# A transformer block with a state-space mixer and a quantised FFN on one core: another order of the steps on three engines, and the last down product in two halves of columns

## What is computed

```
sa, ca, ga, sb, cb, gb = six sections of (silu(c) @ w_mod)      # ga, gb kept at least 0.25 away from 0
h = layernorm(x) * (1 + ca) + sa
x = x + ga * mixer(h)
h = layernorm(x) * (1 + cb) + sb
return x + gb * ffn(h)

mixer(h):  z, xBC, dt = split(h @ W_in.T)            # 1024, 1280 and 16 columns
           dt = softplus(dt + dt_bias)
           x, B, C = split(silu(causal conv of 4 taps over xBC))      # 16 heads of 64; B, C of 128
           y = scan of the state S <- exp(dt*A)*S + dt*B*x, read out by C, plus D*x
           y = y * silu(z);  y = y * rsqrt(mean(y*y) + 1e-5) * norm_w
           return y @ W_out.T
ffn(h):    return (silu(h @ Wg.T) * (h @ Wu.T)) @ Wd.T     # 1408 hidden columns, integer weights with scales
```

## Time and profile before

| | |
|---|---|
| median of 3 runs | 1406.8 us (1405.69 to 1407.49) |
| profiled execution | 1406.29 us, of which the span of its trace is 1404.4 us |
| granted TensorE clock, mean | 0.994 |
| busy: PE, PEld, DVE, ACT, POOL | 99%, 84%, 76%, 55%, 13% |

### The profile page before, as it was taken

The page is one execution under the profiler, slowest core; times in us unless marked ns, Lnnn a source line. Parts: engine busy times, 40 slices in busy tenths (PEclk is TensorE's granted clock), DMA queues, the critical chain, the costliest instruction groups (busy, mean ns, idle before and its releaser), DMA issues.

```text
span 1404.4 us, 26004 instructions
## 1 busy us (share of the span) xinstructions
PE 1385.7 (99%) x9607; PEld 1173.2 (84%) x9607; DVE 1071.5 (76%) x2095; ACT 777.4 (55%) x1782; POOL 185.1 (13%) x270
## 2 busy tenths in 40 slices
PE   8899999999999999999999999999999999999998
PEld 6788888888888888888888888798888888888887
DVE  4888899999999989989989988766645536464542
ACT  5867777787787787787787787522211112021110
POOL 0011111111111111101111111111020110102101
PEclk8999999999999999999999999999999999999999
DMA  8422123223124223122332234522020201202010
GB/s 289 170 79 98 69 100 106 84 89 116 61 77 140 73 76 126 72 91 85 98 106 83 92 98 140 222 98 75 1 90 15 75 31 61 90 0 91 15 45 31
DMA packets 61066, 125.02 MB, mean 89 GB/s; under 512 B 6998, under 2 KB 10626, under 8 KB 60940
## 3 DMA queue, kind: packets, MB, share of 16 engines
q1 hardware_dynamic: 60112, 122.22, 25.4%
q10 hardware_dynamic: 828, 1.12, 0.2%
HBM read 97.62 MB, written 25.69 MB: 88 GB/s over the span
## 4 chain that ended last, share of the span: by engine, by line
PE 90%; issue 4%; DMA 2%; DVE 2%; POOL 1%; ACT 1%; SPq 0%; POOLq 0%; ACTq 0%; DVEq 0%
PE bank L1563 29%; PE bank L2153 19%; PE bank L2183 9%; PE bank L1714 9%; PE bank L56 5%; PE bank L1718 4%; PE bank L1685 4%; PE bank L1649 4%; PE bank L1693 2%; PE bank L1629 2%; PE bank L1553 1%; PE bank L2134 1%; DMA silu_z<-W_inT 1%; POOL ff_x_resid L1980 1%; DMA ff_x_resid<-x_scratch 0%
## 5 line engine op out<-in xcount | busy, mean ns | idle before, releaser
L1988 ACT ACTIVATE silu_gate<-bank,params 128x512 f32<-128x512 f32 (+1 forms) x99 | 63.5, 642 | 363.3 <-PE bank L2153 343.9
L1074 DVE SCALAR_TENSOR_TENSOR xBC<-conv_in,wconv,xBC 128x256 f32<-128x256 f32 x480 | 223.1, 476 | 10.5 <-ACT xBC L782 8.0
L2060 DVE SCALAR_TENSOR_TENSOR hidden<-bank,params,silu_gate 128x512 f32<-128x512 f32 (+1 forms) x99 | 68.3, 690 | 126.7 <-PE bank L2153 126.7
L857 ACT ACTIVATE decay<-decay,sums 128x128 f32<-128x128 f32 x512 | 156.5, 395 | 0.2 <-DMA decay<-sums_scratch 0.2
L2183 PE MATMUL bank<-W_down,hidden_high 128*128 128x512 f32 x374 | 138.9, 390 | 0.0
L2153 PE MATMUL bank<-ff_h_high,W_gate 128*128 128x512 f32 (+1 forms) x352 | 132.1, 379 | 0.0
L700 POOL TENSOR_TENSOR X_D<-X,Drow 128x1024 f32<-128x1024 f32 x32 | 61.7, 1927 | 532.4 <-ACT X_D L871 290.1
L2153 PE MATMUL bank<-ff_h_high,W_up 128*128 128x512 f32 (+1 forms) x352 | 130.9, 376 | 0.3 <-DVE hidden L2060 0.3
L2153 PE MATMUL bank<-ff_h_low,W_gate 128*128 128x512 f32 (+1 forms) x352 | 130.9, 376 | 0.0
L2153 PE MATMUL bank<-ff_h_low,W_up 128*128 128x512 f32 (+1 forms) x352 | 130.9, 376 | 0.0
L2183 PE MATMUL bank<-W_down,hidden_low 128*128 128x512 f32 x330 | 128.4, 389 | 0.0
(11 more groups left out here) (199 smaller groups left out, 3118.4 us busy)
## 6 DMA issues: line engine op xcount, KB each, us to landing
decay<-sums_scratch SPq DMA_DIRECT2D x62, 512.0 KB, 4.8
wq_rows<-wqT SPq DMA_DIRECT2D x33, 256.0 KB, 2.9
widened_scratch<-wq_rows SPq DMA_DIRECT2D x33, 256.0 KB, 2.0
x_tile<-x SPq DMA_DIRECT2D x32, 256.0 KB, 3.3
x_resid<-x SPq DMA_DIRECT2D x32, 256.0 KB, 2.8
x_scratch<-x_resid SPq DMA_DIRECT2D x32, 256.0 KB, 2.0
ff_x_resid<-x_scratch SPq DMA_DIRECT2D x32, 256.0 KB, 4.4
out<-ff_x_resid SPq DMA_DIRECT2D x32, 256.0 KB, 2.0
```

The costliest lines, as they stand in the source:

```text
L857: last = nc.scalar.activation(x[:, h, :], x[:, h, :], ACT.Relu, bias=A.s3[:, o:o + 1], scale=-1.0)
L1074: nc.vector.scalar_tensor_tensor(A.xc[b][:, m, :], A.raw[:, m, j:j + SC], A.wconv[:, m, j:j + 1], A.xc[b][:, m, :], ALU.mult, ALU.add).the ...
L1988: self.nc.scalar.activation(B.sg[m % 2][:, 0:size], self.gates[m % 2][:, 0:size], ACT.Silu, scale=self.T.sgate[:, m:m + 1]).then_inc(self. ...
L2060: nc.vector.scalar_tensor_tensor(hid, self.ups[m % 2][:, 0:size], self.T.sup[:, m:m + 1], B.sg[m % 2][:, 0:size], ALU.mult, ALU.mult).then ...
```

## The change

The three tables get another order in `first()`, `turn()` and `drain()` of TensorE, VectorE and ScalarE; no step is added or dropped in them. In the FFN the last tile of `down` (turn 8, c = 3) is done in two halves of 256 columns, first into bank 7, then into bank 6, with twice as many matmuls of half the width. For this tile VectorE also adds the residual, in place of GpSimd, and SP makes two stores of 128 KB in place of one of 256 KB.

```diff
@@ tensor, first() @@
             n, b = 0, 0
+            setup.turn_params(pe)
             project_zdt(n, 0)
-            setup.turn_params(pe)
             project_zdt(n, 1)
...
             project_tile(n, 9)
-            cumulate(n)
             pe.wait_ge(setup.win_low, len(setup.stage))
             project_z(n, 0)
             project_z(n, 1)
+            cumulate(n)
@@ tensor, drain() @@
             project(0, 3)
+            states(n, u, 0, 0)
             project(0, 4)
-            states(n, u, 0, 0)
             states(n, u, 0, 1)
@@ vector, drain() @@
+            decay_S(u, b, 0, 1)
+            decay_S(u, b, 1, 1)
+            decay_S(u, b, 1, 0)
+            decay_X(n, u, 0)
             gate(n, u, b, 0)
             ff.hidden(dve, 0, 2)
-            decay_X(n, u, 0)
-            decay_S(u, b, 0, 1)
@@ FFN @@
+    def last(self, t, c):
+        return t == self.N - 1 and c == self.NC[t] - 1
+
+    def pieces(self, t, c):
+        D = self.T.D
+        return (slice(0, D // 2), slice(D // 2, D)) if self.last(t, c) else (slice(0, D),)
@@ sync @@
-                wait(sp, self.summed, self.first[t] + c, 1, 1)
-                sp.dma_start(self.rows_of(T.out, t, c), B.xr[c][:]).then_inc(self.out_sent[c], 16)
+                for h, s in enumerate(self.pieces(t, c)):
+                    if self.last(t, c):
+                        sp.wait_ge(self.last_summed, h + 1)
+                    else:
+                        wait(sp, self.summed, self.first[t] + c, 1, 1)
+                    sp.dma_start(self.rows_of(T.out, t, c)[:, s], B.xr[c][:, s]).then_inc(self.out_sent[c], 16)
@@ gpsimd @@
+                if self.last(t, c):
+                    continue
@@ read_down @@
+            if self.last(t, c):
+                wait(dve, self.down_read, self.first[t] + c, 1, h + 1)
+                wait(dve, self.resid_in, self.first[t + 1], 16, 0)
+                self.nc.vector.tensor_tensor(B.xr[c][:, s], B.ob[c % 2][:, s], B.xr[c][:, s], ALU.add) \
+                    .then_inc(self.last_summed, 1)
@@ down @@
-                    mm = nc.tensor.matmul(self.downs[c % 2][:], self.hidden_tile(t, a, m)[:, s].bitcast(dt),
-                                          B.Wd[:, m, :].bitcast(dt), start=(m == 0 and a == 0), stop=(m == KH - 1 and a == 1))
+            for h, d in enumerate(self.pieces(t, c)):
+                if h:
+                    wait(pe, self.down_read, self.first[t] + c, 1, 0)
...
+                        mm = nc.tensor.matmul(self.downs[(c + h) % 2][:, d], self.hidden_tile(t, a, m)[:, s].bitcast(dt),
+                                              B.Wd[:, m, d].bitcast(dt), start=(m == 0 and a == 0),
+                                              stop=(m == KH - 1 and a == 1))
```

More of the change, by code:

```diff
@@ L1028, in drain @@
             ff.silu_gate(act, 0, 9)
+            square(u, 1)
             ff.silu_gate(act, 0, 10)
@@ L1339, in first @@
             conv(n, b, 9, 1)
+            conv(n, b, 8, 2)
+            setup.wout_lo(dve, 2)
             conv(n, b, 9, 2)
             setup.scale_gate(dve)
+            tails(n, b)
             split_h(after(n), n, 0)
-            setup.wout_lo(dve, 1)
-            tails(n, b)
-            split_h(after(n), n, 1)
-            setup.wout_lo(dve, 2)
             setup.wout_lo(dve, 3)
             setup.wout_lo(dve, 4)
+            split_h(after(n), n, 1)
             setup.wout_lo(dve, 5)
@@ L1418, in turn @@
                 sums(n)
+                conv(n, b, 5, 0)
             if bef:
@@ L1457, in turn @@
             if own:
-                conv(n, b, 8, 1)
-                top_square(n)
+                top_square(n)
+                conv(n, b, 6, 2)
+                conv(n, b, 8, 0)
+            if bef:
+                residual(n, u, b, 0)
+            if own:
+                conv(n, b, 8, 1)
+            if bef:
+                low_g(n, u, 1, 0)
+                low_g(n, u, 1, 1)
+            if nxt:
+                norm(after(n), n, 1)
+            if own:
+                conv(n, b, 8, 2)
+                conv(n, b, 7, 0)
+            if bef:
+                decay_S(u, b, 1, 1)
             conv(n, b, 7, 1)
@@ L1512, in drain @@
             ff.hidden(dve, 0, 3)
+            ff.stats(dve, 1, 0)
             read_state(u, b, 0, 1)
             low_g(n, u, 0, 0)
-            ff.stats(dve, 1, 0)
-            ff.norm(dve, 1, 0)
+            low_g(n, u, 0, 1)
+            read_yoff(n, u, b, 1, 0)
+            read_ydiag(n, u, 1, 0)
+            ff.hidden(dve, 0, 4)
             scores(u, 1, 1)
-            low_g(n, u, 0, 1)
-            read_ydiag(n, u, 1, 0)
-            read_yoff(n, u, b, 1, 0)
-            ff.hidden(dve, 0, 4)
             ff.hidden(dve, 0, 5)
@@ L1812, in turn @@
             if bef:
-                states(n, u, 1, 0)
                 transpose_g(n, u, 1, 0)
```

339 lines of the change are left out of this document (156 added, 183 removed).

## The result

The changed kernel takes 1403.92 us at the median of 12 runs (1400.92 to 1407.08), the old one beside it 1406.62 us (12 runs, 1404.58 to 1408.44). The ratio is 0.9981, with a 95% interval of 0.9972 to 0.9989: a gain of 2.7 us.

What follows compares the result with a forecast made beforehand. TensorE, busy 99% of the span, bounds the kernel, with half clock in two stretches; −2.3 − 2.4 − 0.7 − 1.0 = −6.4 us from 1406.29 gives 1399.9, forecast 1400 us; 8-in-10 range 1397.5 to 1405.5.

Steps and rivals of the forecast that it cites:

- the turns: Turns 1 to 15: removing a recurring TensorE wait gives −2.4 us, bounds −3.9 and 0.
- the layout of a turn: Steady turn's steps set out at old distances: out-projection 0.8 us spare, second `y_diag` 0.3, other inputs at least 0.4 early.
- the seam's wait: TensorE between the second transposes of `g` and the out-projection: a wait of 0.11 to 0.16 us per turn goes.
- The sign of being wrong that the prediction named: A turn longer than 53.8 us from its first matmul to the next turn's would prove the prediction wrong.
- The third rival: New waits of 0.13 to 0.4 us a turn, or a late turn 0 transfer: 1402 to 1406 us; chance 0.18.
- the start: Turn 0: `turn_params` moves into idle time and the clock rises sooner, near 23.4 us; −2.3 us, bounds −3 and 0.
- The rival by which the clock would rise where it did: At the start: clock rise not brought forward, gain −0.4 in place of −2.3 us, time 1402; chance 0.16.
- turn 1: The 4.34 us wait before `y_diag` and the half clock behind it stay: 0, bounds −0.7 and +1.2 us.
- the drain: Drain: TensorE's waits for the state and `decay_X` can go, waits for x stay; −0.7 us, bounds −1.3 and +0.5.
- the end: FFN's last tile: shorter chain −1.2, narrow matmuls +0.38, store −0.2; total −1.0 us, bounds −1.4 and −0.6.

Runs made afterwards that it cites:

- r11: Changed kernel with second weights load issued early, first weights load held until the sums' read-back lands, and one last store; ratio 0.9965 to the old kernel.
- r7: Old kernel with only the new turn 0 tables of `first()`; ratio 0.9988 to the old kernel.
- r3: Changed kernel with the old kernel's FFN end (512-column last tile, GpSimd addition, one 256 KB store); ratio 0.9983 to the old kernel.
- r4: Changed kernel with the two halves kept but one last store of 256 KB in place of two of 128 KB; ratio 0.9978 to the old kernel.
- r6: Old kernel with only the new tables for turns 1 to 15; ratio 1.0003 to the old kernel.
- r1: Changed kernel run again without any edit; ratio 0.9974 to the old kernel.
- r2: Changed kernel with SP issuing the second load of integer weights ahead of the residual's store and load; ratio 0.9971 to the old kernel.
- r10: Old kernel with only the new end of the FFN; ratio 0.9995 to the old kernel.

## Why the prediction was right or wrong

**Wrong: the turns.** The step that failed is the layout of a turn, in the sentence "All other inputs come 0.4 us or more early in this layout". It set out steps of TensorE, VectorE and GpSimd, and had no lane for SP's queue and for the landing of its transfers, among them the transfers of instructions. The term was −2.4 us for turns 1 to 15 with bounds of −3.9 and 0; the seam's wait did go in every turn (53.88 to 53.75 us, and turn 2 gave 0.6 us), but turns 3 to 15 became 1.3 us longer together (701.6 against 700.35; 0.8 us by the mean of all six traces with these turns and queue order) where the term has 2 us less. With the loads moved in r11 they are 2.1 us shorter than the old ones, so the term itself was sound for the engines. The sign of being wrong that the prediction named, a turn over 53.8 us, came in turns 3, 4, 8, 10 and 12 of the first trace; turn 4 has 53.89 in r11 too. The old trace had what was needed: the second load of weights was used 4.5 us after its issue, on a queue where it stands behind a store and a load tied to `residual`, and `residual` was one of the steps moved on VectorE. Likewise the read-back of the sums takes 4.8 us at the median, and the decays that use it moved 1.35 us earlier, to 4.7 us behind its issue. The third rival named "a late transfer in turn 0"; the mechanism was right and put at the wrong place. Its time, 1402 to 1406 us with a chance of 0.18, holds the measured 1403.9 us, which lies outside the forecast's own 1398.3 to 1401.8.

**Right in mechanism, a little small: the start.** Both parts came: `turn_params` went into the idle time, and the clock rose 5.3 us after the first projection (18.98 to 24.24), near the 5.1 us of turn 1 in the old trace. (That the inputs of `turn_params` are there from the very start is wrong: L371 waits 1.3 us, the trace names VectorE's L199, and 0.83 us of idle time are left behind it.) With the old turn 0 the half speed ended between 26.1 and 27.9 us in four traces, with the new one between 22.8 and 25.6 in ten; counted from the first projection, 7.9 to 9.6 us and 3.7 to 6.0 us. r7 changed all of turn 0's tables, so it is not shown that the place of `turn_params` alone does this. The −2.3 became −1.7 at turn 1's first matmul in the first pair of traces (61.04 to 59.34) and −1.4 by the means of two and three traces (60.95 to 59.53). What is missing is that the first projection itself began later, at 19.0 us in the mean of ten traces with the new turn 0 against 18.5 in four with the old one; whether the new order does that or the loads' landing is left open. The rival by which the clock would rise where it did is out. The Trainium skill ("TensorE: Matmul & The Clock Gate", "What's actually happening") has the point of the rise vary between runs, by 500 ns to either side. The traces agree that it varies, but by more: the rise lies anywhere in 2.8 us with one order of turn 0. The two orders still do not overlap.

**Too cautious: turn 1.** I took 0 for the stretch at half speed. The wait of 4.3 us stayed (3.8 to 4.4 us in all traces), but the stretch was 3.4 us in five of ten traces with the new turn 0 (6.8 us in the other five and in all four with the old one), and that brings up to 1.7 us more. The changed kernel's three traces all have 3.4 us; but r3 and r4, which are the same as it and as each other up to the FFN, have 6.8 and 3.4, so the order alone does not settle it. The clock is one cause of the spread between executions: in the old kernel's four groups of 17 to 35, mean clock and span go against each other with a correlation of −0.8 to −0.9. In the changed kernel's three groups it is −0.7 to +0.1, so something besides the clock varies there.

**Right, its size in part by luck: the drain,** −0.7 us forecast, −0.78 measured up to the first `down` in the first pair of traces; the waits of 0.87 and 0.25 us became 0.3 and none. But r6 shows that the new turns by themselves make the old drain 0.8 us longer, of which the forecast had nothing, and that the new drain takes this back as well.

**Mis-sized: the end.** The chain came out (−1.2 us, and +0.4 for the narrow matmuls), the store did not: "A store of 128 KB should land a little earlier than 2.0 us" is true in three traces (1.7 us in r1, 1.8 in r2) and false in four (3.4 us in the changed kernel's first). The mean tail of seven traces is 4.5 us in place of 4.9, so the end gives about 0 to 0.7 us in place of 1.0 (r10: 0.7, r3 against r1: 1.3 by the ratios, both with wide intervals).

**The sum** by the means of the traces (old two, changed three; a minus is time won): turn 2's start −2.1, turn 2 −0.6, turns 3 to 15 +1.3, drain and FFN with the narrow matmuls −0.4, tail −0.4; together −2.2 us, against 2.7 to 3.7 us by the times. Of the 4.2 us between that and the forecast's 6.4, the turns' transfers are 3.3 (13 × 0.15 not won and 1.3 lost), the end 1.0 and the start with turn 1 0.5, and turn 2 and the drain are 0.5 us better than forecast.

## What to carry to other kernels

When a step is moved, lay out the DMA queue like an engine: for every transfer, what its issue waits for in an in-order queue, and how many microseconds lie between issue and use, against the median and the longest landing of its kind. Ask also which turns have the long landings, for they need not be chance: here they were the same turns in six traces, those with a packet of instructions beside the load. A cover that shrinks from 4.5 us to between 3.2 and 3.7, for a transfer that takes 2.8 us at the median and 4.1 to 5.1 beside such a packet, costs nothing in most turns and 2.6 us in one, and since ScalarE has the next turn's first decays behind it, TensorE pays all of it. A gain by a tighter order is worth only what the transfers' slack leaves, and the remedy may be on the queue alone, at no cost to any engine.

## What the runs showed of the hardware that I had not expected

- A transfer of instructions shares the DMA engines with the data: one packet of 16 KB beside a 256 KB load in turns 2 to 14 goes with a landing of 4.1 to 5.1 us in place of 2.7 to 3.0 (78 loads in six traces, no overlap), and beside the last store's packets with 3.4 to 4.0 us in place of 1.7 to 2.2.
- The same read-back of 512 KB took between 3.6 and 6.7 us to land in one trace of the changed kernel, with a median of 4.8. The old kernel's took 3.7 to 6.8: the scatter was there, and the cover was 6.2 us and not 4.7.
- `sums`, 32 elements on VectorE, took 1.14 us beside GpSimd's multiplication in turn 5 where it took 1.70: it is done when GpSimd is, and it was only started later. The multiplication itself took 2.06 us in place of 1.90.
- After the same stop of TensorE in turn 1 the half speed lasted 3.4 us in r4 and 6.8 in r3, two kernels that are the same up to the FFN.
